# Router work of a fused attention and expert kernel: chosen behind the leaky passes, rows normalised at the end of a step, first expert products ahead of later takes

## The chip, the cores and the metric

One Trainium2 chip, one of its cores. The metric is the device time of one execution in microseconds. The core has five engines that run their own instruction queues in order and meet at semaphores: TensorE (PE in the profile), VectorE (DVE), ScalarE (ACT), GpSimd (POOL) and SyncE (SP), and 16 DMA engines.

## What is computed

A graph attention layer over 2048 nodes of width 128, then a layer of 64 experts of which each node uses two. Both add to their input.

```
x = x + attention(layernorm(x), adj)          # 2048 nodes, width 128
x = x + experts(layernorm(x))

attention: h = n @ W.T + b_W
           e[i,j] = leaky(h_i . a1 + h_j . a2 + b_a)     # slope 0.2
           softmax over j where adj[i,j] > 0, times h
experts:   logits = n @ Wr + br ; top 2 of 64 ; gates = softmax of the two
           out = sum over the two of gate * (relu(n @ W1[e] + b1[e]) @ W2[e] + b2[e])
```

## The kernel before

**Attention.** The nodes are 16 tiles of 128 (T = 16). Everything is unrolled, and each engine's order is written out by hand; the loop over s from 0 to 15 is a step on each engine. For tile s, VectorE makes the masked scores (L747), ScalarE their lower branch (`scores`, L560 to L564), VectorE the smaller of both in step s+1 (`leaky`, L753). TensorE transposes the result (`turn`, L1015) into four PSUM banks, ScalarE evacuates these with the exponential (`evac`, L576, four instructions, in its step s+1), TensorE multiplies by h (`attend`, L1039, 16 pairs of instructions with j from 0 to 15), and VectorE adds the result to x (`residual`, L757 and L761, in its step s+3). VectorE also makes the penalty of the next tile (L738). The scores live in a ring of three buffers, the transposed ones in a ring of two.

**Norm of the rows.** ScalarE sums the squared deviation of a finished tile (`deviation`, L583, step s-3). GpSimd makes from it the scale and shift of two tiles (`rstd_of`, L411 to L416, four operations, in even steps s). ScalarE writes the normalised rows twice (`norm`, L589). Before, tiles 2i and 2i+1 are normalised in step 5 + 2i, ahead of `evac`.

**Router.** The tiles form seven groups (START = 0, 4, 8, 10, 12, 14, 15, 16); LAST[q] is a group's last tile: 3, 7, 9, 11, 13, 14, 15. Per group: `route_a` on TensorE transposes the rows (L1049) and on ScalarE copies them out (L596); `route_b` on TensorE makes the logits (L1055, L1058) and on ScalarE one exponential (L601); `top2` on VectorE finds the two experts (first instruction L768, MAX8; last L782); `route_c` on TensorE ranks the nodes within their expert (L1078); `place` on VectorE makes gates and table positions (L789 to L800). GpSimd then writes each tile's rows into a table in memory, two indirect DMAs per tile (`place`, L431), in the steps that PLACED lists or after the loop, and loads the adjacency tiles (L377). `EARLY` is the number of groups handled inside the loop.

The order on VectorE in step s is

```
scores(s) ; penalty(s+1) ; residual(s-3) ; [top2(q) if s == LAST[q]+5] ; leaky(s-1) ; [place(q) if s == LAST[q]+5]
```

On ScalarE a step is scores(s), deviation(s-3), norms, route_b, evac(s-1), with the copy of route_a between the second and third bank of evac. On TensorE `route_a(q)` and `route_b(q)` stand at the start and a quarter into attend(LAST[q]+3), and `route_c(q)` ahead of turn(LAST[q]+4).

**Experts.** After the router, GpSimd gathers 34 blocks of 64 rows as 17 pairs (L480), TensorE transposes a gathered pair (`take`, L1135), ScalarE copies it out (`x_evac`, L649), and 96 steps, each one block with one expert, follow: `up` (L1146), relu halves on ScalarE (L654) and VectorE (L900), `down` (L1158), accumulation on VectorE (L907). ScalarE also copies the expert's weights (`fetch`, L662). `up(p)` waits until block pair min(p, 32)//2 + 1 has been copied out by `x_evac`. TensorE starts with take(0), take(1), up(0), up(1).

## Time and profile before

| | us |
|---|---|
| runs: median of 3 | 276.71 |
| runs: lowest, highest | 275.14, 277.4 |
| the profiled execution | 275.16 |
| its span, first to last instruction | 273.4 |
| mean granted TensorE clock | 0.926 of full |
| busy: TensorE, VectorE | 227.0, 208.4 |
| busy: ScalarE, GpSimd | 180.2, 167.0 |

The profile is of one execution. An engine is busy while an instruction of it runs; waits are not counted. Successive instructions of one engine overlap slightly, so the distance between two starts is what an instruction costs its engine. A wait is shown with the instruction that ended it. A row of a timeline gives start, duration, engine, line, operation, output and inputs, shape, count, and in brackets the idle time ahead of it with what ended it. A row of windows gives the stretch, its length, the busy time (and count of instructions) of TensorE, its weight loads, VectorE, ScalarE and GpSimd, the granted TensorE clock as a share of 2.4 GHz, the share of the DMA engines that was busy, and GB/s.

### The profile page before, as it was taken

To read this page: it belongs to the slowest core of one execution; us is meant where nothing else is said; L and a number is where in the kernel's file an instruction comes from. 1 tells how busy PE (TensorE), PEld (TensorE's weight loads), DVE (VectorE), ACT (ScalarE), POOL (GpSimd) and SP (SyncE) were. 2 spreads that over 40 slices of the span, in tenths; PEclk is the share of its full clock that TensorE was granted. 3 is DMA by queue.
4 is the path that set the end of the run, shared out by engine and by line. 5 is a ranking of instruction groups with operands and counts; after the bars stand their busy time and mean duration, and the time that the engine had idled before them with its cause. 6 is when DMAs were issued, how large, how long until landed. Compare 5 with 4: busy or idle time off the path is not lost.

```text
span 273.4 us, 6241 instructions
## 1 busy us (share of the span) xinstructions
PE 227.0 (83%) x1863; PEld 215.0 (79%) x1863; DVE 208.4 (76%) x587; ACT 180.2 (66%) x425; POOL 167.0 (61%) x212
## 2 busy tenths in 40 slices
PE   1494899999699966978884749999999999999840
PEld 1354899999689966978773639999999999999740
DVE  6879999996999799699455505889886766676465
ACT  2748989999298947758334336887877777777300
POOL 5770003450899889778577753455888888866500
PEclk9999799999799999799995557999999999999995
DMA  6988665589429817108931122222168701100067
GB/s 155 210 161 152 129 119 79 159 228 236 120 66 284 229 39 272 41 10 320 418 120 39 51 63 66 71 66 63 46 185 295 246 31 38 35 31 22 31 198 273
DMA packets 11120, 36.89 MB, mean 135 GB/s; under 512 B 2256, under 2 KB 2832, under 8 KB 10320
## 3 DMA queue, kind: packets, MB, share of 16 engines
q0 software_dynamic: 5232, 14.98, 24.1%
q1 hardware_dynamic: 5424, 21.11, 22.6%
q10 hardware_dynamic: 432, 0.40, 0.7%
q8 instruction: 17, 0.28, 0.4%
q14 instruction: 15, 0.12, 0.1%
HBM read 39.36 MB, written 5.51 MB: 164 GB/s over the span
## 4 chain that ended last, share of the span: by engine, by line
PE 60%; DVE 15%; POOL 7%; DMA 7%; issue 5%; ACT 3%; SPq 1%; POOLq 0%; DVEq 0%; ACTq 0%
PE bank L1146 17%; PE bank L1158 16%; PE bank L1039 12%; PE bank L1015 8%; DVE arena L753 5%; POOL table L431 5%; DMA xs<-in_x 2%; DMA arena<-result 2%; PE bank L980 2%; PE bank L1135 2%; PE bank L1058 1%; PE bank L1055 1%; DMA rows_in<-table,arena 1%; DVE idx L773 1%; DVE hot L779 1%
## 5 line engine op out<-in xcount | busy, mean ns | idle before, releaser
L1039 PE MATMUL bank<-arena 128*128 128x130 f32 x512 | 61.5, 276 | 0.0
L1146 PE MATMUL bank<-arena 128*128 x384 | 60.9, 283 | 0.1
L1039 PEld LDWEIGHTS bank<-arena 128*128 128x128 f32 x512 | 59.5, 192 | 0.5 <-ACT arena L576 0.3
L1158 PE MATMUL bank<-w2s,arena 128*128 x384 | 59.2, 277 | 0.2 <-issue 0.2
L431 POOL DMA_INDIRECT table<-rows_in,pos x32 | 48.7, 1522 | 8.9 <-issue 8.5
L1146 PEld LDWEIGHTS bank<-arena 128*128 128x128 f32 x384 | 52.0, 197 | 0.6 <-issue 0.3
L1158 PEld LDWEIGHTS bank<-w2s,arena 128*128 128x128 f32 x384 | 51.0, 193 | 0.6 <-issue 0.6
L907 DVE SCALAR_TENSOR_TENSOR arena<-bank,arena 128x128 f32 x96 | 33.6, 350 | 22.3 <-PE bank L1158 21.0
L654 ACT ACTIVATE arena<-bank,arena 128x128 f32<-128x128 f32 x96 | 35.1, 366 | 19.0 <-PE bank L1146 17.7
L1015 PE MATMUL bank<-ident,arena 128*128 128x128 f32 x256 | 35.5, 299 | 12.9 <-DVE arena L753 12.9
L576 ACT ACTIVATE arena<-bank 128x512 f32<-128x512 f32 x64 | 34.0, 597 | 14.9 <-PE bank L1015 14.6
L1015 PEld LDWEIGHTS bank<-ident,arena 128*128 128x128 f32 x256 | 32.0, 154 | 14.4 <-DVE arena L753 14.4
L662 ACT ACTIVATE arena<-arena 128x256 f32 x96 | 39.0, 408 | 2.3 <-issue 2.2
L494 POOL DMA_INDIRECT result<-arena x33 | 33.6, 1017 | 9.2 <-POOL arena L492 8.9
L900 DVE TENSOR_SCALAR arena<-bank,arena 128x128 f32<-128x128 f32 x96 | 33.2, 346 | 7.6 <-PE bank L1146 7.4
L753 DVE SCALAR_TENSOR_TENSOR arena<-arena,tneg 128x2048 f32<-128x2048 f32 x16 | 37.5, 2348 | 0.0
L747 DVE CUSTOM_DVE_ANT_0 arena<-arena 128x2048 f32<-128x2048 bf16 x16 | 36.7, 2301 | 0.9 <-ACT arena L516 0.9
L564 ACT ACTIVATE arena<-arena,c_lo 128x2048 f32<-128x2048 f32 x16 | 32.0, 2003 | 0.5
L480 POOL DMA_INDIRECT rows_in<-table,arena x17 | 16.1, 946 | 17.7 <-PE bank L1135 15.1
L377 POOL DMA_DIRECT2D arena<-in_adj x16 | 9.3, 584 | 26.0 <-DVE arena L738 25.7
L492 POOL TENSOR_SCALAR arena<-arena 128x128 f32<-128x128 f32 x32 | 19.6, 614 | 6.9 <-DVE arena L907 5.7
L411 POOL TENSOR_SCALAR nm<-total 128x2 f32<-128x2 f32 (+1 forms) x9 | 5.8, 649 | 16.5 <-ACT off L583 16.3
(195 smaller groups left out, 282.1 us busy)
## 6 DMA issues: line engine op xcount, KB each, us to landing
arena<-in_adj POOLq DMA_DIRECT2D x16, 512.0 KB, 6.6
w2s<-in_w SPq DMA_DIRECT2D x8, 768.0 KB, 4.5
arena<-in_w SPq DMA_DIRECT2D x6, 1024.0 KB, 9.3
arena<-in_w SPq DMA_DIRECT2D x4, 512.0 KB, 4.7
w2s<-in_w SPq DMA_DIRECT2D x4, 512.0 KB, 3.9
xs<-in_x SPq DMA_DIRECT2D x4, 256.0 KB, 6.5
arena<-result SPq DMA_DIRECT2D x2, 512.0 KB, 4.4
arena<-result SPq DMA_DIRECT2D x4, 256.0 KB, 5.9
```

The source lines that it names most:

```text
L431: pool.indirect_dma_start(table[:, :], bass.IndirectOffsetOnAxis(pos[:, t, k:k + 1], 0), rows_out[:, t, k, :].bitcast(I32), None).then_inc ...
L494: pool.indirect_dma_start(result[:, :], bass.IndirectOffsetOnAxis(slot_id[:, b:b + 1], 0), y_all[:, b, :], None).then_inc(e_put, 16)
L576: act.activation(pt_r[:, t % 2, CB * b:CB * b + CB, :].rearrange("p c i -> p (c i)"), bank[b][:, :], ACT.Exp, scale=-1.0).then_inc(s_ea, 1)
L654: act.activation(hT[:, p % UH, 0, :], hp(p, 0), ACT.Relu, bias=b1p[:, 0, p:p + 1]).then_inc(e_ha, 1)
L662: act.activation(w1u[:, p % UW, :], w1s[:, bass.ds(u, 1), :].rearrange("p e h -> p (e h)"), ACT.Copy).then_inc(e_w, 1)
L747: dve.tensor_tensor_reduce(out=z_r[:, t % 3, :], in0=pen[:, t % 2, :], in1=trow[:, :], scale=1.0, scalar=HIGHEST, op0=ALU.add, op1=ALU.min ...
L753: dve.scalar_tensor_tensor(z, z, tneg[:, t:t + 1], low(t), ALU.subtract, ALU.min).then_inc(s_lk, 1)
L907: dve.scalar_tensor_tensor(y, yp(p), mask[:, p:p + 1], y, ALU.mult, ALU.add).then_inc(e_acc, 1)
L1015: ins = pe.transpose(bank[b][:, P * c:P * c + P], z_r[:, t % 3, P * j:P * j + P], ident[:, :])
L1039: ins = pe.matmul(OB[t % 2][:, 0:D + 2], pt_r[:, t % 2, j, :], h[:, j, :], start=(j == 0), stop=(j == T - 1))
L1146: ins = pe.matmul(hp(p, b), w1u[:, p % UW, P * b:P * b + P], xT_all[:, bass.ds(column, P)], start=True, stop=True)
L1158: ins = pe.matmul(yp(p), hT[:, p % UH, b, :], w2s[:, bass.ds(u, 1), b, :].rearrange("p e d -> p (e d)"), start=(b == 0), stop=(b == HB - 1))
```

## The change

- `place(2, 8)` and `place(2, 9)` leave step 15 of GpSimd's loop; they go after the loop, one ahead of `rstd_of(6)` and one behind it. `EARLY` becomes 4, so group 3 is handled by the same loops.
- ScalarE normalises tiles s-4 and s-3 at the end of every even step s, after `evac(s-1)`: one step sooner than before. The copy of `route_a(q)` goes to step LAST[q]+4, after the deviation and ahead of `evac`; `route_b(q)` of ScalarE to the end of that step.
- VectorE runs `top2(q)` one step sooner (LAST[q]+4) and behind `leaky(s-1)` instead of ahead of it. `place(q)` stays in step LAST[q]+5 behind the leaky pass.
- TensorE runs `route_a(q)` at j = 8 of attend(LAST[q]+2), `route_b(q)` behind that product, and `route_c(q)` behind attend(LAST[q]+3).
- In the experts, TensorE runs take(0), up(0), up(1), take(1), down(0), up(2), take(2), and then the old loop from p = 1; ScalarE runs `x_evac(1)` behind `relu(0)`.

```diff
--- before.py
+++ after.py
@@ -23,9 +23,8 @@
     SLOT = [0, GRP, 0, 2, GRP, GRP + 2, GRP + 3]
     COUNTED = 2
     LAST = [START[q + 1] - 1 for q in range(NG)]
-    PLACED = [(0, 0, 9), (0, 1, 10), (0, 2, 11), (0, 3, 11), (1, 4, 13), (1, 5, 13), (1, 6, 13), (1, 7, 15), (2, 8, 15), (2, 9, 15)]
-    EARLY = 3
-    NORMED = [(5 + 2 * i, 2 * i) for i in range(5)]
+    PLACED = [(0, 0, 9), (0, 1, 10), (0, 2, 11), (0, 3, 11), (1, 4, 13), (1, 5, 13), (1, 6, 13), (1, 7, 15)]
+    EARLY = 4
     LNS = [(t, t + 2) for t in range(0, T - 2, 2)] + [(T - 2, T - 1), (T - 1, T)]
     CB = 4
     ROW = D + 2
@@ -456,7 +455,9 @@
                 for q in range(COUNTED):
                     if s == LAST[q] + 5:
                         counts(q)
+            place(2, 8)
             rstd_of(6)
+            place(2, 9)
             rstd_of(7)
             for t in (10, 11):
                 place(3, t)
@@ -565,9 +566,6 @@
 
             def evac(t):
                 for b in range(4):
-                    for q in range(NG):
-                        if b == 2 and q < EARLY and t == LAST[q] + 3:
-                            route_a(q)
                     if t == T - 1 and b == 2:
                         deviation(T - 2)
                     act.wait_ge(s_pt, 4 * t + b + 1)
@@ -608,20 +606,17 @@
                                   padrow[:, 1:1 + TOPK, :].rearrange("p j w -> p (j w)").bitcast(I32)).then_inc(d_tail, 16)
                 if s >= 3:
                     deviation(s - 3)
-                for at, t in NORMED:
-                    if s == at:
-                        norm(t)
-                        norm(t + 1)
                 for q in range(EARLY):
-                    if s == LAST[q] + 5:
-                        route_b(q)
-                if s == T - 1:
-                    route_a(3)
+                    if s == LAST[q] + 4:
+                        route_a(q)
                 if s >= 1:
                     evac(s - 1)
-                if s == T - 2:
-                    norm(T - 6)
-                    norm(T - 5)
+                if s >= 4 and s % 2 == 0:
+                    norm(s - 4)
+                    norm(s - 3)
+                for q in range(EARLY - 1):
+                    if s == LAST[q] + 4:
+                        route_b(q)
             deviation(T - 3)
             route_b(3)
             norm(T - 4)
@@ -668,9 +663,10 @@
                 fetch(p)
             act.wait_ge(s_b1, 1)
             x_evac(0)
-            x_evac(1)
             for p in range(PAIRS):
                 relu(p)
+                if p == 0:
+                    x_evac(1)
                 if p % 2 == 1 and p // 2 + 2 < NG2:
                     x_evac(p // 2 + 2)
                 if p + UW - 1 < PAIRS:
@@ -829,11 +825,10 @@
                     penalty(s + 1)
                 if s >= 3:
                     residual(s - 3)
-                for q in range(EARLY):
-                    if s == LAST[q] + 5:
+                leaky(s - 1)
+                for q in range(EARLY - 1):
+                    if s == LAST[q] + 4:
                         top2(q)
-                leaky(s - 1)
-                for q in range(EARLY):
                     if s == LAST[q] + 5:
                         place(q)
             leaky(T - 1)
@@ -1018,18 +1013,13 @@
             def attend(t):
                 if t >= 2:
                     pe.wait_ge(s_x1, t - 1)
-                for q in range(EARLY):
-                    if t == LAST[q] + 3:
-                        route_a(q)
-                if t == T - 2:
-                    route_b(3)
                 if t == T - 1:
                     route_a(4)
                 for j in range(T):
                     b = j // CB
                     for q in range(EARLY):
-                        if j == T // 4 and t == LAST[q] + 3:
-                            route_b(q)
+                        if j == 8 and t == LAST[q] + 2:
+                            route_a(q)
                     if t == T - 1 and j == 8:
                         route_b(4)
                     if t == T - 1 and j == 12:
@@ -1038,6 +1028,9 @@
                         pe.wait_ge(s_ea, 4 * t + b + 1)
                     ins = pe.matmul(OB[t % 2][:, 0:D + 2], pt_r[:, t % 2, j, :], h[:, j, :], start=(j == 0), stop=(j == T - 1))
                 ins.then_inc(s_o, 1)
+                for q in range(EARLY):
+                    if t == LAST[q] + 2:
+                        route_b(q)
 
             def route_a(q):
                 pe.wait_ge(s_row, START[q + 1])
@@ -1079,15 +1072,11 @@
                 ins.then_inc(s_rk, 1)
 
             for s in range(T):
-                for q in range(EARLY):
-                    if s == LAST[q] + 4:
-                        route_c(q)
                 turn(s)
                 attend(s)
-                if s == T - 3:
-                    route_a(3)
-                if s == T - 2:
-                    route_c(3)
+                for q in range(EARLY):
+                    if s == LAST[q] + 3:
+                        route_c(q)
             route_c(4)
             route_b(5)
             route_c(5)
@@ -1164,12 +1153,15 @@
             blocks = load_words(pe, "pe_b", 0, 0, WORDS)
             slots = load_words(pe, "pe_u", 1, 0, WORDS)
             take(0)
-            take(1)
             up(0)
             up(1)
+            take(1)
             pe.wait_ge(s_mask, 1)
             pe.wait_ge(s_b1, 1)
-            for p in range(PAIRS):
+            down(0)
+            up(2)
+            take(2)
+            for p in range(1, PAIRS):
                 if p % 2 == 0 and p // 2 + 2 < NG2:
                     take(p // 2 + 2)
                 if p + 2 < PAIRS:
```

## Rows read from the trace of the kernel before

**Rows 1.** Windows, the first four between starts of VectorE's steps (columns above).
```profile
55.25:60.81 5.56, 5.56 (x53) 5.56 (x52) 5.52 (x9) 5.44 (x10) 3.37 (x4) 1.00 0.93 254
60.81:74.11 13.30, 11.24 (x97) 10.47 (x97) 10.35 (x32) 8.43 (x17) 6.05 (x11) 0.93 0.65 151
...
90.90:103.39 12.49, 10.36 (x96) 9.47 (x95) 10.41 (x32) 8.02 (x18) 10.84 (x13) 1.00 0.43 115
...
109.07:120.67 11.60, 10.03 (x74) 9.66 (x75) 8.74 (x26) 7.02 (x15) 8.91 (x9) 0.85 0.10 30
...
72.10:75.60 3.50, 3.44 (x17) 3.44 (x18) 3.36 (x9) 1.79 (x3) 3.01 (x7) 0.52 0.65 216
```

**Rows 2.** Timeline of VectorE: start us, us, instruction [idle before <-releaser].
```profile
47.43 2.35 DVE L753 SCALAR_TENSOR_TENSOR arena<-arena,tneg 128x2048 f32<-128x2048 f32 x1
...
66.82 0.63 DVE L768 MAX8 top<-bank 128x8 f32<-128x64 f32 x4 [2.64 <-PE bank L1058]
...
69.76 2.35 DVE L753 SCALAR_TENSOR_TENSOR arena<-arena,tneg 128x2048 f32<-128x2048 f32 x1
72.02 0.16 DVE L789 TENSOR_SCALAR gs<-ge 128x4 f32<-128x4 f32 x1
...
74.11 2.40 DVE L747 CUSTOM_DVE_ANT_0 arena<-arena 128x2048 f32<-128x2048 bf16 x1
...
96.03 0.63 DVE L768 MAX8 top<-bank 128x8 f32<-128x64 f32 x4 [1.77 <-PE bank L1058]
...
114.99 0.36 DVE L768 MAX8 top<-bank 128x8 f32<-128x64 f32 x2 [2.55 <-PE bank L1058]
```

**Rows 3.** Timeline of ScalarE over one step and the norms of the next.
```profile
48.22 0.32 ACT L560 ACTIVATE r<-tneg,s 128x1 f32<-128x1 f32 x1
...
50.80 0.39 ACT L583 ACTIVATE off<-xs,total 128x128 f32<-128x128 f32 x1
...
51.19 1.08 ACT L589 ACTIVATE rows_in<-xs,nm,rstd 128x256 f32<-128x256 f32 x2
52.17 2.02 ACT L576 ACTIVATE arena<-bank 128x512 f32<-128x512 f32 x4
```

**Rows 4.** Timeline of TensorE: a clean step, group 0's router product, a later wait.
```profile
56.55 1.91 PE L1015 MATMUL bank<-ident,arena 128*128 128x128 f32 x16
58.29 3.75 PE L1039 MATMUL bank<-arena 128*128 128x130 f32 x32
61.87 1.91 PE L1015 MATMUL bank<-ident,arena 128*128 128x128 f32 x16
...
65.05 0.70 PE L1055 MATMUL bank<-bss,ones_f 1*128 1x256 f32 x2
...
135.51 0.41 PE L1049 MATMUL bank<-ident,rows_in 128*128 128x128 f32 x2 [1.12 <-issue]
```

**Rows 5.** Timeline of GpSimd: chains of statistics (L411 to L416) and table writes (L431).
```profile
47.98 1.86 POOL L416 TENSOR_TENSOR nm<-nm,rstd 128x2 f32<-128x2 f32 x1
...
74.55 2.98 POOL L431 DMA_INDIRECT table<-rows_in,pos  x1 [0.18 <-issue]
...
86.85 0.86 POOL L411 TENSOR_SCALAR nm<-total 128x2 f32<-128x2 f32 x1
...
89.18 1.85 POOL L416 TENSOR_TENSOR nm<-nm,rstd 128x2 f32<-128x2 f32 x1
...
131.69 0.96 POOL L431 DMA_INDIRECT table<-rows_in,pos  x1 [0.30 <-issue]
...
134.09 0.20 POOL L416 TENSOR_TENSOR nm<-nm,rstd 128x2 f32<-128x2 f32 x1
```

**Rows 6.** Timeline at the start of the experts, ScalarE and TensorE.
```profile
162.44 0.38 ACT L649 ACTIVATE arena<-bank 128x256 f32<-128x256 f32 x1 [0.16 <-PE bank L1135]
...
162.95 0.69 PE L1135 MATMUL bank<-ident,rows_in 128*128 128x128 f32 x2 [0.60 <-DMA rows_in<-table,arena]
...
163.43 1.91 PE L1146 MATMUL bank<-arena 128*128 x8
```

## The prediction

> **What bounds the kernel now.** I read the busy shares first, then the busy time between the starts of VectorE's steps, then each engine's timeline over two such steps, and last the chain of waits. Over 20 to 129 us the kernel runs 16 attention steps, and VectorE sets their pace. A step without router work lasts 5.56 us, with VectorE busy for 5.52 of it, TensorE for 5.56 and ScalarE for 5.44 [rows 1]: three engines are nearly full, VectorE has no slack, and neither of the others can make up much. A leaky pass costs 72.02 - 69.76 = 2.27 us of it [rows 2]; scores (2.2), penalty and residual make up the other 3.3. The three steps with a routed group are the long ones: 13.30, 12.49 and 11.60 us [rows 1]. VectorE waits in them for the logits: 2.64, 1.77 and 2.55 us ahead of the first MAX8 [rows 2], 6.96 in all. Its own router work is 69.76 - 66.82 = 2.94 us for the choice and 74.11 - 72.02 = 2.09 for the placing of four tiles [rows 2], which the change moves but does not shorten. TensorE's step is a turn (1.75 us) and an attention product (3.58): 5.33 us from 56.55 to 61.87 [rows 4]. ScalarE's step is 2.6 for scores, 0.4 for the deviation and 1.9 for four evacuations, 4.9 us; two norms add 1.0 us every second step [rows 3]. So ScalarE needs 10.8 us of every 11.1. GpSimd looks idle at first, but from 74.5 us on it is a queue of table writes [rows 5].
>
> **Part 1, the norms moved to the end of the even steps (ScalarE).** Before, the statistics of a pair were made on GpSimd one whole step ahead of the norms. Now norm(s-4) and norm(s-3) stand in the very step whose deviation(s-3) starts GpSimd's chain. That chain has four operations; for tiles 0 and 1 the last of them starts at 47.98, 0.55 us into a leaky pass of VectorE (47.43 to 49.70), and takes 1.86 us, to 49.84 [rows 2, 5]. The same operation takes 0.20 where no leaky pass runs, at 134.09 [rows 5]. ScalarE's evacuations end at 48.22 [rows 3], so it now stands until 49.9, and norms to 50.9. What is queued behind the wait: the next scores, the evacuation of the next turn, and through it TensorE's product. In numbers: scores(5) start at 50.9 instead of 48.22, its last result is ready at 53.55, so leaky(5) starts 0.6 late (VectorE could at 47.43 + 5.55 = 52.98); evac(4) starts at 53.94 instead of 52.17 [rows 2, 3], and attend(4) 0.7 behind it at 54.7.
>
> The Trainium skill (SBUF — State Buffer, "SBUF: two separate sides") says that VectorE and GpSimd share a pair of ports as an exclusive lock, and that a VectorE operation with two SBUF inputs, as the leaky pass is, blocks a GpSimd operation that reads SBUF until it ends. The trace agrees (1.86 us against 0.20). With the lock the first norm wait is 1.7 us, without it 0.
>
> **Part 2, the choice of group 0 behind leaky(6).** I follow it on. leaky(5) ends at 55.87, leaky(6) at 61.42. attend(4) ends at 58.25, turn(5) runs to 60.0, evac(5) on ScalarE from 58.9 to 60.8, deviation(3) ends at 58.9. GpSimd's chain for tiles 2 and 3 begins at 59.0, meets leaky(6) (59.15 to 61.42) and ends at about 62.7; norm(3) is done at 63.7. TensorE stands in the middle of attend(5) (its eighth tile is reached at 61.8) for these rows until 63.85, transposes (0.44), ends the product at 66.1. ScalarE's copy of the transposed rows stands behind scores(7) (2.6) and deviation(4) (0.4 to 0.5): 63.7 + 3.1 + 0.5 = 67.3. Then the router product, begun at 65.05 before and followed by the MAX8 at 66.82, 1.75 us [rows 2, 4]: 69.1. VectorE, free at 61.4, starts top2(0) at 69.1: it waits 7.7 us where it waited 2.64. From there 2.94 + 5.55 + 2.09 gives 79.7 for the start of step 9, which was 74.11 [rows 2]. **Group 0: +5.6 us.** TensorE's next turn and product lie beside this, hence the cover that the change uses; but VectorE, not TensorE, is what later steps wait for, so that cover gives nothing back.
>
> **Part 3, group 1.** It is the same chain, but GpSimd now comes to the statistics of tiles 6 and 7 only after four table writes and two adjacency loads. Before, these ran from 74.55 to 86.85, and the chain from there to 91.03 (89.18 + 1.85) [rows 5]; I keep the 12.3 us, because a write beside a busy VectorE takes up to 2.98 against 0.96 beside an idle one [rows 5]. Place(0) now ends at 79.7; GpSimd still counts group 0, so the writes start at 81.1, the chain at 93.4, it ends at 97.6 behind leaky(10). ScalarE would be free at 93.5 and stands 4.1 us. Norms to 98.6, scores(11) and deviation(8) and the copy to 102.1, router product to 103.8. VectorE has ended leaky(10) at 96.4: it waits 7.5 us (1.77 before). Step 13 starts at 103.9 + 2.94 + 5.55 + 2.09 = 114.5 instead of 103.39 [rows 1]. **Group 1: +5.5.**
>
> **Part 4, group 2.** Here place(1) (2.09) stands between the leaky pass that frees the turn and the choice, GpSimd is idle, and the group has two tiles. By the same chain the logits are ready 1.2 us after leaky(12) instead of 2.55 late: step 15 starts at 130.3 instead of 120.67 [rows 1], +9.6 in all. **Group 2: -1.5.**
>
> **Part 5, group 3 and the table writes moved.** The norms of tiles 10 and 11 wait for GpSimd behind the six writes of tiles 4 to 6 (114.8 to 130.0 by 3.2 us each beside a busy VectorE and 1.26 beside an idle one), which costs TensorE another 1.4 us in the product of tile 13. Moving place(2, 9) behind rstd_of(6) takes two writes of 1.26 from ahead of norm(12), and the 1.12 us for which TensorE stood ahead of route_a(4) at 135.51 vanish [rows 4]. It comes there at 145.3 and, with its product no longer held up behind it, to route_b(4) 9.5 later than before. From there nine writes of GpSimd, the last being the padding, set the end as before. **Tail: -0.1.**
>
> **Part 6, the experts' start.** take(1) waited for its gathered block until 162.95 and up(0), up(1) began at 163.43 [rows 6]. Now up(0) needs only x_evac(0), which started at 162.44 and took 0.38 [rows 6], so it starts at 162.9. The transposes of takes 1 and 2 are the same work, later in the queue. down(0) moves ahead of up(2) and take(2): relu(0) is long done, and relu(1) behind x_evac(1) is done before down(1). The fifth gather waits for take(1), some 1.8 us later than now, and its block is wanted only by take(4), four expert steps on. The loop after it is bound by TensorE, so what is gained at the start stays. **-0.5** (0 if ScalarE's new order costs it, -1 if the slow stretch, in which eight products take 1.91 us [rows 6], also ends sooner).
>
> **Sum.** 275.16 (the profiled execution, of which 273.4 is the span) + 5.6 + 5.5 - 1.5 - 0.1 - 0.5 = 284.2. The median of the runs, 276.71, is 1.55 above that execution; I take half of it and predict 285.0.
>
> **Clock.** TensorE waited for the choice of group 0 and for leaky(7), and the next turn was granted 0.52 (near 1.2 GHz): 3.44 us busy instead of 1.75 [rows 1, 4]. With the same waits around group 1 the clock stayed at 1.00 [rows 1]. The new waits of TensorE (2.0 and 1.3 us at group 0, 4.0 and 1.3 at group 1) may halve the router product's speed: up to 1.6 us for each of two groups. I take 0 in the sum and +3.2 as the upper bound.
>
> [...]
>
> **Rivals.** A: *GpSimd's chain is not held up* (the leaky pass misses it, or writes are quicker). Then only ScalarE's order counts: norm(3) ends at 60.4, copy at 64.0, logits at 65.7, and group 0 costs +2.2; group 1 at 3.5 us of waiting against 1.77 costs +1.7; with -1.3, -0.1 and -0.5 the time is 277.2. The rows with 1.86 and 2.98 us [rows 5] speak against it. B (the other side): *the choice is ready almost when the leaky pass ends*, as it would be were ScalarE never late. TensorE alone needs 1.75 + 3.58 + 0.6 + 1.75 = 7.7 us from a leaky pass, against VectorE's 5.55: waits of 2.1, 2.1 and 0 instead of 6.96 in all, so -2.8, and -0.5: 271.9. It decides from the point at which group 0's logits come before 61.4 + 2.64 = 64.0. The 3.1 us of scores and deviation ahead of the copy [rows 3] speak against it: even a norm that waits for nothing gives 64.0 for the copy alone. C: *the changes of order cancel*, waits about as long as before: 274 to 279. D: *the clock falls too*: 287 to 289.
>
> **Chances.** My forecast (281 to 287) 0.52; A (277 to 281) 0.20; C 0.10; D 0.11; B 0.07. The range leaves out B, half of C and the far end of D: 277.0 to 289.0. A measurement of this kernel tells 1% (2.8 us) from no change: over 1% faster takes B, 0.07; within 1% takes C and a small part of A, 0.14; slower 0.79.
>
> **What would show it.** In the changed kernel's trace: VectorE's idle time ahead of the first MAX8 of groups 0 and 1 at 5 to 8 us each and about 1 for group 2; ScalarE idle ahead of L589's norms, released by GpSimd, for 1 to 2 us at first and about 4 in step 10; a gap in TensorE's product of step 5. If those norms wait for nothing, part 1 is wrong and A holds. If the MAX8 waits add up to less than 7 us, the forecast is wrong in sign. An up(0) that does not start before the second take makes part 6 nothing.

## The result, and the profile after

The changed kernel takes 287.25 us (median of 4 runs, 285.59 to 289.4) against 275.92 before: a ratio of 1.0451, 95% interval 1.0313 to 1.0589. It is slower, as forecast; 285.0 was predicted, with 277 to 289. Here and below a median takes all runs of a kernel, while a ratio leaves out those more than 1.5% above its fastest. Its profiled execution took 285.81 us, with a span of 284.0 against 273.4, so 10.6 us are to be found between two traces.

VectorE first, as in [rows 2]: its timeline in the changed kernel (start us, us, instruction, in brackets the wait ahead of it and what ended it). L743 is the scores, L749 the leaky pass, L764 the choice.

```profile
47.57 2.38 DVE L749 SCALAR_TENSOR_TENSOR arena<-arena,tneg 128x2048 f32<-128x2048 f32 x1
49.87 2.28 DVE L743 CUSTOM_DVE_ANT_0 arena<-arena 128x2048 f32<-128x2048 bf16 x1
...
53.72 2.35 DVE L749 SCALAR_TENSOR_TENSOR arena<-arena,tneg 128x2048 f32<-128x2048 f32 x1 [0.48 <-ACT arena L565]
...
68.86 0.63 DVE L764 MAX8 top<-bank 128x8 f32<-128x64 f32 x4 [7.22 <-PE bank L1051]
...
79.54 2.28 DVE L743 CUSTOM_DVE_ANT_0 arena<-arena 128x2048 f32<-128x2048 bf16 x1
...
103.37 0.63 DVE L764 MAX8 top<-bank 128x8 f32<-128x64 f32 x4 [6.99 <-PE bank L1051]
...
114.07 2.28 DVE L743 CUSTOM_DVE_ANT_0 arena<-arena 128x2048 f32<-128x2048 bf16 x1
...
121.60 0.36 DVE L764 MAX8 top<-bank 128x8 f32<-128x64 f32 x2 [1.80 <-PE bank L1051]
...
130.59 2.28 DVE L743 CUSTOM_DVE_ANT_0 arena<-arena 128x2048 f32<-128x2048 bf16 x1
...
136.95 2.35 DVE L749 SCALAR_TENSOR_TENSOR arena<-arena,tneg 128x2048 f32<-128x2048 f32 x1 [1.33 <-ACT arena L565]
```

The waits for the logits are 7.22, 6.99 and 1.80 us where [rows 2] has 2.64, 1.77 and 2.55: 16.0 in place of 7.0. The start of step 9 is 79.54 against 74.11 (0.17 of the difference was there at step 6 already), that of step 13 114.07 against 103.39, that of step 15 130.59 against 120.67.

What ends those waits is read on ScalarE and TensorE. First ScalarE's timeline in the changed kernel.

```profile
50.03 1.10 ACT L587 ACTIVATE rows_in<-xs,nm,rstd 128x256 f32<-128x256 f32 x2 [0.89 <-POOL nm L415]
...
62.53 1.09 ACT L587 ACTIVATE rows_in<-xs,nm,rstd 128x256 f32<-128x256 f32 x2 [1.49 <-POOL nm L415]
...
66.46 0.57 ACT L594 ACTIVATE x2T<-bank 128x512 f32<-128x512 f32 x1
...
96.47 1.09 ACT L587 ACTIVATE rows_in<-xs,nm,rstd 128x256 f32<-128x256 f32 x2 [2.84 <-POOL nm L415]
```

And TensorE's:

```profile
63.67 0.66 PE L1042 MATMUL bank<-ident,rows_in 128*128 128x128 f32 x4 [1.63 <-ACT rows_in L587]
...
67.09 0.70 PE L1048 MATMUL bank<-bss,ones_f 1*128 1x256 f32 x2 [0.96 <-ACT x2T L594]
...
97.61 0.66 PE L1042 MATMUL bank<-ident,rows_in 128*128 128x128 f32 x4 [2.98 <-ACT rows_in L587]
98.11 3.42 PE L1029 MATMUL bank<-arena 128*128 128x130 f32 x16
...
112.00 3.62 PE L1010 MATMUL bank<-ident,arena 128*128 128x128 f32 x16 [2.93 <-DVE arena L749]
...
145.91 0.38 PE L1042 MATMUL bank<-ident,rows_in 128*128 128x128 f32 x2
```

Group 0 reads as a chain: the norms wait for GpSimd (L415) until 62.53, TensorE stands in the middle of its product until 63.67 for these rows, the copy (L594) comes only at 66.46 behind the scores and the deviation, and TensorE waits for it again. In [rows 3] no norm waited. At 98.11 the second half of the product takes 3.42 us where 1.96 is usual, and the turn at 112.00 3.62 against the 1.91 of [rows 4]. The windows between VectorE's steps (columns as in [rows 1]) show the granted clock of these stretches at 0.87 to 0.89; over the slow product alone (98.11 to 101.53) it is 0.54, over the slow turn (112.00 to 115.62) 0.53:

```profile
90.74:106.32 15.58, 12.60 (x93) 11.71 (x92) 8.42 (x25) 8.92 (x19) 9.44 (x10) 0.89 0.63 172
106.32:114.07 7.75, 4.82 (x45) 4.69 (x45) 7.58 (x16) 3.64 (x7) 1.97 (x6) 0.87 0.13 28
```

GpSimd's timeline has the cause of the first waits. L413 is the power and L415 the product that ends the statistics, the one of 47.98 in [rows 5].

```profile
47.61 0.72 POOL L413 TENSOR_TENSOR rstd<-ve,expo 128x2 f32<-128x2 f32 x1
48.41 1.59 POOL L415 TENSOR_TENSOR nm<-nm,rstd 128x2 f32<-128x2 f32 x1
...
59.58 2.64 POOL L413 TENSOR_TENSOR rstd<-ve,expo 128x2 f32<-128x2 f32 x1
62.30 0.20 POOL L415 TENSOR_TENSOR nm<-nm,rstd 128x2 f32<-128x2 f32 x1
```

The experts start like this on TensorE, with the last `down` product of the stage; [rows 6] has the same place before.

```profile
171.65 0.69 PE L1124 MATMUL bank<-ident,rows_in 128*128 128x128 f32 x2 [3.00 <-DMA rows_in<-table,arena]
173.15 2.07 PE L1135 MATMUL bank<-arena 128*128 x8 [0.81 <-ACT arena L644]
...
178.91 0.71 PE L1135 MATMUL bank<-arena 128*128 x4 [0.27 <-ACT arena L657]
...
266.57 0.71 PE L1147 MATMUL bank<-w2s,arena 128*128 x4 [0.20 <-issue]
```

The first take is at 171.65 against 161.66 (+10.0) and the last product at 266.57 against 256.10 (+10.5). So the router's part costs 10.0 and the experts' start another 0.5; the last 0.1 of the 10.6 come behind the last product.

### The profile page after: what moved, and what is told of

It reads as the page before. It is cut to its first block, busy times and chain, and to the rows that moved or that the text cites. A ratio compares the mean times of both kernels' runs of the same rounds, so it can differ in the third digit from the quotient of the medians.

```text
span 284.0 us, 6243 instructions
## 1 busy us (share of the span) xinstructions
PE 229.9 (81%) x1863; PEld 218.5 (77%) x1863; DVE 208.7 (73%) x587; ACT 180.5 (64%) x425; POOL 156.7 (55%) x212
## 4 chain that ended last, share of the span: by engine, by line
PE 51%; DVE 12%; POOL 11%; issue 9%; ACT 8%; DMA 7%; SPq 1%; POOLq 0%; ACTq 0%; DVEq 0%
PE bank L1135 16%; PE bank L1147 15%; PE bank L1029 6%; PE bank L1010 6%; POOL table L430 4%; DVE arena L743 3%; DVE arena L749 2%; DMA xs<-in_x 2%; DMA arena<-result 2%; ACT rows_in L587 2%; POOL rstd L413 2%; PE bank L975 2%; ACT arena L574 2%; PE bank L1051 2%; PE bank L1124 1%
## 5 line engine op out<-in xcount | busy, mean ns | idle before, releaser
L1029 PE MATMUL bank<-arena 128*128 128x130 f32 x512 | 64.0, 283 | 1.0 <-ACT arena L574 1.0
L1029 PEld LDWEIGHTS bank<-arena 128*128 128x128 f32 x512 | 62.3, 199 | 1.2 <-issue 1.2
L1135 PEld LDWEIGHTS bank<-arena 128*128 128x128 f32 x384 | 51.4, 195 | 2.4 <-issue 2.2
L1010 PE MATMUL bank<-ident,arena 128*128 128x128 f32 x256 | 37.3, 309 | 13.2 <-DVE arena L749 13.2
L430 POOL DMA_INDIRECT table<-rows_in,pos x32 | 41.2, 1289 | 8.8 <-issue 8.3
L1010 PEld LDWEIGHTS bank<-ident,arena 128*128 128x128 f32 x256 | 34.0, 161 | 14.2 <-DVE arena L749 14.2
L749 DVE SCALAR_TENSOR_TENSOR arena<-arena,tneg 128x2048 f32<-128x2048 f32 x16 | 37.6, 2350 | 1.8 <-ACT arena L565 1.8
L743 DVE CUSTOM_DVE_ANT_0 arena<-arena 128x2048 f32<-128x2048 bf16 x16 | 36.5, 2285 | 0.3 <-ACT arena L517 0.3
L764 DVE MAX8 top<-bank 128x8 f32<-128x64 f32 x16 | 2.8, 222 | 21.0 <-PE bank L1051 21.0
(195 smaller groups left out, 281.5 us busy)
```

The costliest lines, as they stand in the source:

```text
L430: pool.indirect_dma_start(table[:, :], bass.IndirectOffsetOnAxis(pos[:, t, k:k + 1], 0), rows_out[:, t, k, :].bitcast(I32), None).then_inc ...
L743: dve.tensor_tensor_reduce(out=z_r[:, t % 3, :], in0=pen[:, t % 2, :], in1=trow[:, :], scale=1.0, scalar=HIGHEST, op0=ALU.add, op1=ALU.min ...
L749: dve.scalar_tensor_tensor(z, z, tneg[:, t:t + 1], low(t), ALU.subtract, ALU.min).then_inc(s_lk, 1)
L1010: ins = pe.transpose(bank[b][:, P * c:P * c + P], z_r[:, t % 3, P * j:P * j + P], ident[:, :])
L1029: ins = pe.matmul(OB[t % 2][:, 0:D + 2], pt_r[:, t % 2, j, :], h[:, j, :], start=(j == 0), stop=(j == T - 1))
L1135: ins = pe.matmul(hp(p, b), w1u[:, p % UW, P * b:P * b + P], xT_all[:, bass.ds(column, P)], start=True, stop=True)
```

## The experiments

**The two halves of the change.** Is the loss in the router alone, and does the new start of the experts bring or cost something? Two kernels: the one before with the experts' edit (on TensorE as below, and `x_evac(1)` behind `relu(0)` on ScalarE), and the changed one without it.

```diff
             take(0)
-            take(1)
             up(0)
             up(1)
+            take(1)
...
+            down(0)
+            up(2)
+            take(2)
-            for p in range(PAIRS):
+            for p in range(1, PAIRS):
```

> The kernel before with only the experts' new start (take(1) behind up(1), down(0), up(2), take(2), x_evac(1) behind relu(0)). Read within the expert stage, from the start of the first take to the last down product: 94.44 us before, 94.92 in the changed kernel. Theory: ScalarE, which now copies block 1 between relu(0) and the weight copies, falls behind, up(4) waits for a weight copy (0.27 us in the changed kernel) and the stage takes 94.8 to 95.0. Rival, the prediction's part 6: the stage takes 93.9, and the 0.48 us lost in the changed kernel came from the phase in which the router work left the stage. The first MAX8 waits stay at 2.64, 1.77 and 2.55.

Measured: from the first take at 162.40 to the last product at 257.65 it is 95.25 us, against 256.10 - 161.66 = 94.44 before. The start costs 0.8 us, a little more than the theory's 0.4 to 0.6, and the rival's gain of 0.5 is excluded. The kernel took 276.92 us (one execution). The waits ahead of the first MAX8 were 3.24, 2.97 and 2.55 in this execution, so those of the kernel before vary by over a microsecond as well.

> The changed kernel with the old start of the experts, so the router's part alone. Theory: all of the slowdown but 0.5 us is here; its profiled span is 283.3 to 283.8, the ratio to the kernel before 1.035 to 1.045, and VectorE waits 7.2, 7.0 and 1.8 us ahead of the first MAX8 of groups 0, 1, 2. Rival (the experts' start costs some of the loss by its order and by a clock that rises later): ratio 1.02 to 1.03.

Measured: 289.1 us against 277.26, ratio 1.0433 (1.0352 to 1.0515), and 94.45 us from first take to last product, as before. So the router's part carries the slowdown. The profiled span missed, 288.9 instead of 283.3 to 283.8 (it is the longest of the four runs, 287.57 to 290.66): VectorE waited 5.87, 6.41 and 1.25 us for the logits, but 2.67 and 3.76 ahead of two leaky passes for which the changed kernel's profile has 0.48 and 1.33. That opened a question of its own, taken up with e10 and e11.

TensorE's timeline of e1 shows where the start loses: the first products begin 1.49 us behind the first take (1.77 before, [rows 6]), and then `up(4)` waits for a weight copy on ScalarE, which now copies a gathered block between `relu(0)` and its weight copies. That is only part of the 0.8 us: the instruction ahead, `up(3)` at 168.52, is already 0.51 us late, 6.12 us behind the first take against 167.27 - 161.66 = 5.61 before. The lower clock lasted longer here. The granted clock was 0.50 and 0.54 over `up(2)` and the take behind it, which took 1.01 and 0.40 us from start to start; in the changed kernel it was 0.67 and 1.00 there, and they took 0.77 and 0.22.

```profile
163.89 2.07 PE L1147 MATMUL bank<-arena 128*128 x8 [0.81 <-ACT arena L649]
...
167.11 1.22 PE L1147 MATMUL bank<-arena 128*128 x4
168.12 0.57 PE L1136 MATMUL bank<-ident,rows_in 128*128 128x128 f32 x2
...
170.07 0.71 PE L1147 MATMUL bank<-arena 128*128 x4 [0.27 <-ACT arena L662]
```

**Which part of the chain makes the wait.** The forecast had GpSimd's statistics and ScalarE's order in series. One kernel takes away what the norms wait for, one moves the copy, one does both.

```diff
             def norm(t):
+                if t < 12:
+                    act.activation(rows_out[:, t, :, 0:D],
+                                   xs[:, t, :].rearrange("p (k d) -> p k d", k=1)
+                                   .to_broadcast([P, TOPK, D]), ACT.Identity,
+                                   bias=lift[:, 0:1], scale=1.0).then_inc(s_row, 1)
+                    return
                 act.wait_ge(s_nm2, t // 2 + 1 if t < T - 1 else T // 2 + 1)
```

> The changed kernel in which the rows of tiles 0 to 11 are copied with a constant shift and scale 1 instead of the layer norm's (that part of the computation is left out), so ScalarE's norms inside the loop wait for nothing from GpSimd; GpSimd still makes its statistics. Theory (two causes in series, GpSimd's chain and ScalarE's order): the norm waits of 0.9, 1.5 and 2.8 us vanish, and VectorE's waits ahead of the first MAX8 fall from 7.2 and 7.0 to 4.3 to 5.0 and 3.5 to 4.5, group 2's stays at 1 to 1.8; the kernel comes out 4 to 6 us under the changed one. Rival (ScalarE's order alone sets the wait): the waits fall by less than 1 us each. Rival (GpSimd alone): they fall to 2.1, what TensorE alone needs.

Measured: waits of 4.34, 4.71 and 1.20 us, span 277.1 (278.88 us), 6.9 under the changed kernel and more than expected, since leaky(5) is no longer held either and leaky(15) only by 0.34. Group 1's 4.71 lies just above the expected 4.5. Between these two executions GpSimd's statistics account for about two thirds of the loss of 10.6.

```diff
             for s in range(T):
+                for q in range(EARLY):
+                    if s == LAST[q] + 4:
+                        route_a(q)
                 scores(s)
...
-                for q in range(EARLY):
-                    if s == LAST[q] + 4:
-                        route_a(q)
                 if s >= 1:
                     evac(s - 1)
```

> The changed kernel in which ScalarE copies the transposed rows at the start of its step, ahead of scores and deviation instead of behind them. Theory: in group 0 the copy moves from 66.46 to about 64.3 but TensorE then has to end its product (66.0) before the logits, so they come 1.0 us sooner, VectorE's wait is 6.2 instead of 7.2; group 1 likewise, where the second half of the product ran at the low clock to 101.46 and the copy was done by 101.0: no gain, 7.0. Group 2: about 1.0 less. In all 1 to 2.5 us under the changed kernel. Rival (the copy behind the scores is the main cause): 2 us less in each of two groups, 4 us or more in all.

Measured: 6.18 and 6.89, as expected for groups 0 and 1; 1.87 in group 2, where a shorter wait was expected and none came. The span is 281.5 (283.23 us), 2.5 under the changed kernel; only 1.1 of this is in the two waits for the logits, and 1.8 arise from step 15 to the first take (39.29 us against 41.06), which the expectation did not have. The copy's place matters, but behind late norms it can give little.

> The changed kernel with both earlier edits: norms of tiles 0 to 11 with a constant shift and scale (the layer norm of these rows is left out), and the copy of the transposed rows ahead of the scores on ScalarE. Theory: the two causes stand in series, so with both gone only TensorE's own order is left: VectorE waits 2.5 to 3.5 us ahead of the first MAX8 of groups 0 and 1 and 0 to 1 in group 2, which is still more than the kernel before waits, and the span is about 273 to 275. Rival (a further cause): the waits stay above 4.

Measured: span 272.2 (273.96 us), a little under the expected 273 to 275, and waits 3.80, 2.24 and 0.67 (the bracketed numbers of VectorE's timeline, here of e3 and then e7):

```profile
65.43 0.63 DVE L769 MAX8 top<-bank 128x8 f32<-128x64 f32 x4 [4.34 <-PE bank L1056]
...
97.68 0.63 DVE L769 MAX8 top<-bank 128x8 f32<-128x64 f32 x4 [4.71 <-PE bank L1056]
```

```profile
63.78 0.62 DVE L769 MAX8 top<-bank 128x8 f32<-128x64 f32 x4 [3.80 <-PE bank L1056]
...
93.53 0.62 DVE L769 MAX8 top<-bank 128x8 f32<-128x64 f32 x4 [2.24 <-PE bank L1056]
```

Their sum is 6.7 us, within 0.3 of the kernel before: with both causes gone, the order of the changed kernel has gained nothing that shows in these waits. (Two other executions of the router as it was before, in e1 and e8, have 8.8 and 9.1, so a gain of some 2 us can't be excluded from one execution.) The span is 11.8 under the changed kernel, more than the 6.9 and 2.5 of the two edits alone, as two causes in series would give it. Group 0's 3.80 missed the expected 2.5 to 3.5. There TensorE never stood for rows: it started turn(5) at 56.09, 1.8 us behind the end of leaky(5), since it still worked off what it was behind, and then its turn, product and logits took their full time. This is the floor that rival B of the prediction put at 2.1.

**How long GpSimd's statistics take.** In the changed kernel the power (L413) started 0.04 us behind the start of a leaky pass and took 0.72; in e2 it started 0.05 behind one and took 2.88. Two looks: one small instruction more on GpSimd ahead of that power, and the changed kernel once more.

```diff
                 pool.wait_ge(s_ve2, i + 1)
+                if i == 0:
+                    pool.tensor_scalar(spare[:, :], pidx[:, :], 2.0, None, ALU.mult)
```

> The changed kernel with one small instruction more on GpSimd, 128x1 elements, ahead of the power of rstd_of(0) (L413 in the changed kernel), some 0.2 us. In the changed kernel that power started 0.04 us into a leaky pass and took 0.72; in e2 it started 0.05 us into it and took 2.88. Theory (a GpSimd instruction that comes once a leaky pass is under way stands until the pass ends): the power now starts 0.2 to 0.3 us into leaky(4) and takes over 2 us, the norm of tiles 0 and 1 waits 2.5 to 3.2 us instead of 0.89, leaky(5) 2 to 2.7 instead of 0.48, and step 7 starts 1.5 to 2.3 us later. Rival (the long power of e2 had another cause): the norm waits 1.1 us, 0.2 more than before.

Measured: 291.38 us, span 289.6. GpSimd's timeline in e10:

```profile
47.47 2.39 POOL L415 TENSOR_SCALAR spare<-pidx 128x1 f32<-128x1 f32 x1
49.82 2.80 POOL L416 TENSOR_TENSOR rstd<-ve,expo 128x2 f32<-128x2 f32 x1
```

VectorE's in e10 (L752 leaky, L746 scores):

```profile
47.43 2.35 DVE L752 SCALAR_TENSOR_TENSOR arena<-arena,tneg 128x2048 f32<-128x2048 f32 x1
49.69 2.28 DVE L746 CUSTOM_DVE_ANT_0 arena<-arena 128x2048 f32<-128x2048 bf16 x1
...
56.61 2.35 DVE L752 SCALAR_TENSOR_TENSOR arena<-arena,tneg 128x2048 f32<-128x2048 f32 x1 [3.55 <-ACT arena L568]
```

The small instruction itself stood until the leaky pass had ended, 2.39 us for 128 numbers, and the power behind it fell into the next scores pass and took 2.80. The norm waited 3.94 us, leaky(5) 3.55, and step 7 began at 58.88 instead of 55.98: a delay of 2.9 us, above the 2.3 expected, from an instruction of a few tenths. The direction and the cause are the theory's; its size was taken too small because I had not counted the scores pass as a second one to stand behind.

> The changed kernel once more, to see how far its waits vary by themselves. Theory: VectorE's waits ahead of the first MAX8 stay within 1.5 us of 7.2, 7.0 and 1.8, their sum with the waits of leaky(5) and leaky(15) is 16 to 21 us, and the time follows that sum. Rival: the waits are the same to 0.2 us and the spread of the runs lies elsewhere.

Measured: 289.55 us, span 287.8, with waits of 5.87, 6.54 and 1.62 for the logits and 2.68 and 3.76 ahead of leaky(5) and leaky(15): 20.5 in all where the first profile has 17.8. GpSimd's timeline there:

```profile
46.56 2.88 POOL L413 TENSOR_TENSOR rstd<-ve,expo 128x2 f32<-128x2 f32 x1
```

And VectorE's:

```profile
46.51 2.35 DVE L749 SCALAR_TENSOR_TENSOR arena<-arena,tneg 128x2048 f32<-128x2048 f32 x1
```

The same program thus falls into a short or a long case. The recorded start of the power does not tell which: at 0.05 us into a leaky pass it took 0.72 us in e1 and e5 and 2.88 in e2 and e11, at 0.04 it took 0.72 in the changed kernel's first profile and 2.88 in e8. What settles it within these hundredths stays open.

The first power makes only part of the 3.8 us of span. Counted from the first scores, step 15 comes 1.1 us later in e11; another 3.0 lie between step 15 and the first take, 44.07 us against 41.06 (the first scores come 0.6 sooner). There GpSimd meets the passes a second time. The fifth of the six table writes of step 13 began at 123.46 in the first profile, 0.02 us ahead of a scores pass, and took 0.96; in e11 it began 0.18 into that pass and took 2.94. The sixth took 3.05 instead of 1.89, the power of tiles 10 and 11 2.86 instead of 0.72, and ScalarE's norms waited 3.75 for it where they had waited for nothing. This is behind the 3.76 ahead of leaky(15), 1.33 in the first profile. e2 and e10 have long waits ahead of both passes too (2.67 and 3.76, 3.55 and 3.76), e4 has neither (0.47 and 0.78). Whether the first meeting brings about the second is not shown.

TensorE's timeline in e11 at group 1 shows one more difference: behind the same wait of 2.98 us the second half of the product takes 1.96 us, at a granted clock of 1.00, and not 3.42.

```profile
98.78 0.65 PE L1042 MATMUL bank<-ident,rows_in 128*128 128x128 f32 x4 [2.98 <-ACT rows_in L587]
99.27 1.96 PE L1029 MATMUL bank<-arena 128*128 128x130 f32 x16
```

**The same idea, without taking the step away.** If only VectorE's waits count, the leaky pass can cover them while everything else keeps its step.

```diff
+                leaky(s - 1)
                 for q in range(EARLY):
                     if s == LAST[q] + 5:
                         top2(q)
-                leaky(s - 1)
-                for q in range(EARLY):
-                    if s == LAST[q] + 5:
                         place(q)
```

> The kernel before with one edit: in VectorE's step LAST+5 the leaky pass runs first and the choice and the placing behind it, everything else as it was (norms, products and copies keep their steps). Theory (what VectorE waits for is the logits, and only its own sum of work and waits sets the pace): the leaky pass of 2.27 us covers the wait; ahead of the first MAX8 0.3 to 0.6, 0 and 0.2 to 0.4 us are left instead of 2.64, 1.77, 2.55, and about 0.5 us per group is new ahead of the ranks' product (L794); step 15 starts 4.5 to 5.3 us sooner. TensorE stands longer ahead of its turn and catches up. Of this 2 to 4.5 us reach the end, because GpSimd loses the quiet stretches in which it writes the table fast. Rival (GpSimd's queue is the bound ahead of norm(12)): less than 1 us reaches the end. Rival (TensorE's later turn makes it the bound): VectorE waits 1 to 2 us in the steps behind each group and the gain is 0.

Measured: the waits fell to 0.99, 0 and 0 us, with 0.19 new ahead of the ranks' product in groups 0 and 1 where 0.5 was expected. From the first scores to step 15 it is 95.1 us against 100.1, so 5.0 gained between two executions (it is 102.2 in e1 and 102.6 in e8, whose router is that of the kernel before). But the kernel takes 274.29 against 275.26, ratio 0.9961 (0.9922 to 1.0): the first rival was right on the end. GpSimd's timeline in e5:

```profile
115.10 2.89 POOL L431 DMA_INDIRECT table<-rows_in,pos  x1 [0.30 <-issue]
118.02 1.97 POOL L411 TENSOR_SCALAR nm<-total 128x2 f32<-128x2 f32 x1
```

ScalarE's in e5:

```profile
121.35 1.09 ACT L589 ACTIVATE rows_in<-xs,nm,rstd 128x256 f32<-128x256 f32 x2 [5.04 <-POOL nm L416]
```

VectorE's in e5:

```profile
125.02 2.35 DVE L753 SCALAR_TENSOR_TENSOR arena<-arena,tneg 128x2048 f32<-128x2048 f32 x1 [5.12 <-ACT arena L564]
```

The sixth write of step 13 ends at 118.0, only then can the statistics of tiles 10 and 11 start, ScalarE's norms wait 5.04 us for them, and VectorE's last leaky pass 5.12 for ScalarE: what was gained is given back.

The next two kernels move table writes. The change's own move is put to the kernel before and to e5; then writes are put behind the statistics that are waited for.

```diff
-(1, 7, 15), (2, 8, 15), (2, 9, 15)]
+(1, 7, 15)]
...
+            place(2, 8)
             rstd_of(6)
+            place(2, 9)
             rstd_of(7)
```

> The kernel before with only the table writes of tiles 8 and 9 moved as in the changed kernel. Theory: rstd_of(6) comes about 2.5 us sooner, the 1.12 us for which TensorE stands ahead of route_a(4) vanish, the two writes fill GpSimd's idle 2.56 us; the span from the start of step 15 to the first take is 0.8 to 1.2 us shorter than 40.99. Rival: the later writes push the end of the table, and nothing is gained.

Measured: from the start of step 15 at 122.08 to the first take at 161.34 it is 39.26 us against 40.99, so 1.7 shorter: more than expected, because group 4's first MAX8 waits 2.79 instead of 4.69. The 40.99 is steady: e1, with the old writes, has 162.40 - 121.41 = 40.99 too. Within its stretch this part of the change pays. The whole kernel took 274.44 us in its one execution, inside the spread of the kernel before (273.02 to 277.42).

> The last kernel with the changed kernel's other move as well: the table writes of tiles 8 and 9 leave step 15 and stand around the statistics of tiles 12 and 13. Theory: GpSimd no longer holds norm(12); 4 to 5.5 us under the kernel before, ratio 0.980 to 0.986. Rival (the writes only come later and set the end): the same as the kernel without this move, or slower.

Measured: 270.23 against 275.26 us, ratio 0.9804 (0.9744 to 0.9865), span 267.7. The six runs go from 268.49 to 274.31, and the ratio leaves out the upper two. The theory's 0.980 to 0.986 was met.

> e6 beside e9 on one chip. Theory: ratio to the kernel before again 0.974 to 0.987, and above e9's by 0.002 to 0.007.

Measured: 272.39 against 275.11 us, 268.9 to 275.11 over its runs. Its profile (275.11 us, span 273.4) shows the 5.04 and 5.11 us of e5 again; the first profile of e6 had 1.11 and 1.01 there. The ratio, 0.9798 (0.9754 to 0.9841), leaves out three of the six runs, 273.94, 274.67 and 275.11 us, of which the last is the profiled one. They belong to the kernel all the same, and in them it is no faster than e5, whose ten runs lie at 271.53 and from 273.75 to 275.04. (That the other long runs of e6 have the same wait is not shown: they have no trace.) By the medians e6 is at 0.982 of the kernel before here and 0.990 in e12. The expected order of the ratios missed: e12's is 0.002 below e9's and not 0.002 to 0.007 above.

```diff
-(1, 6, 13), (1, 7, 15)]
+(1, 6, 15), (1, 7, 15)]
...
-            place(2, 8)
             rstd_of(6)
+            place(2, 8)
             place(2, 9)
```

> The kernel e6 with GpSimd's order changed once more: the table writes of tile 6 go from step 13 to step 15, and those of tiles 8 and 9 both stand behind rstd_of(6). Theory (what e5 lost again and e6 kept in part is GpSimd's statistics waiting behind its own table writes): the norms of tiles 10 and 11 wait for nothing or under 1.2 us, leaky(15) is not held, norm(12) comes 1 to 1.5 us sooner; 0.5 to 2 us under e6, and the runs lie closer together. Rival (the writes are only put off to where they set the end of the table): no gain or 1 us slower than e6.

Measured: 269.75 against 275.11 us, ratio 0.9819 (0.9788 to 0.9851), with all six runs between 268.81 and 270.82. The norms of tiles 10 and 11 (118.07 below) wait for nothing, and no leaky pass waits. VectorE's timeline in e9, the choice of groups 2 and 3:

```profile
112.79 0.36 DVE L770 MAX8 top<-bank 128x8 f32<-128x64 f32 x2 [0.26 <-PE bank L1058]
124.93 0.36 DVE L770 MAX8 top<-bank 128x8 f32<-128x64 f32 x2 [0.25 <-PE bank L1058]
```

ScalarE's in e9:

```profile
118.07 1.11 ACT L591 ACTIVATE rows_in<-xs,nm,rstd 128x256 f32<-128x256 f32 x2
...
128.23 1.09 ACT L591 ACTIVATE rows_in<-xs,nm,rstd 128x256 f32<-128x256 f32 x2 [2.45 <-POOL nm L416]
```

By its ratio it is no faster than e6, and the expected 0.5 to 2 us under e6 holds for the medians alone (269.75 against 270.23 and 272.39, so 0.5 and 2.6): none of its six runs has the length of those with the 5 us wait. norm(12) came at 128.23, hardly sooner than e6's 128.55, so there the gain of 1 to 1.5 us was not had. This kernel beats both the one before and the changed one, by 5.4 and 17.5 us of median. Each beside its own runs of the kernel before, their ratios are 0.9819 and 1.0451.

## Why the prediction was right, point by point

- **What bounds the kernel.** VectorE's sum of work and waits: right. Step 13 starts 10.7 us later than before, and of these 9.8 are longer waits for the logits of groups 0 and 1, 0.48 is leaky(5)'s and 0.17 was there at step 6, which leaves 0.2 to everything else.
- **Part 1.** The norm waits were forecast as 1.7 and 1.9 us and measured as 0.89 and 1.49, leaky(5) 0.6 late and measured 0.48. Right in place; the size depends on when GpSimd meets the leaky pass, as e11 (3.06 in the first) and e10 (3.94) showed. The first wait was about half the forecast in this execution and nearly twice it in e11.
- **Part 2, group 0.** The times on the way were forecast within 0.3 us: the first MAX8 at 69.1 (68.86), the start of step 9 at 79.7 (79.54). The waits were forecast less closely, the norm's 1.9 against 1.49 and VectorE's 7.7 against 7.22, and two errors cancelled: the norms were done 0.2 sooner and the start of the attention 0.17 later.
- **Part 3, group 1.** Step 13 was forecast at 114.5 and came at 114.07, for reasons that partly differ. GpSimd's writes began at 82.88 and not 81.1, since two small sums of its count had taken 2.77 us and not the 0.69 of the kernel before. The four writes and two loads then took 9.4 us (82.88 to 92.25) and not 12.3: the first write began 0.04 us ahead of a leaky pass and took 1.13 instead of 2.98, the second 1.82 instead of 2.90. So ScalarE stood 2.84 and not 4.1. Against that, TensorE after its wait of 2.98 us ran the second half of the product at the lower clock, 3.42 instead of 1.96 us, for which I had put 0 into the sum. In e11 the same product behind the same wait took 1.96, so this cost does not come in every execution. The Trainium skill (TensorE: Matmul & The Clock Gate, "Why this matters for your kernels") names idle gaps of TensorE as a cause of lower throughput. The traces agree only in part: slow stretches do stand behind waits, but the length of the wait alone does not tell which, by e11 and by the rows of the last section.
- **Part 4, group 2.** Forecast -1.5, measured 16.52 - 17.28 = -0.76, since turn(11) took 3.62 us at the lower clock and the logits came 1.80 and not 1.2 late (VectorE's wait 0.75 us shorter than before, and not 1.35).
- **Part 5, the tail.** From the start of step 15 to the first take 41.06 against 40.99: +0.07 where -0.1 stood. TensorE came to route_a(4) at 145.91, forecast 145.3. The way there was another, and that it came out so close is luck: the norms of tiles 10 and 11 waited for nothing, where they were to wait for GpSimd's six writes, and instead leaky(15) waited 1.33 us. In e11 those norms did wait, 3.75 us, and the stretch took 44.07.
- **Part 6, the experts.** This term failed in sign: -0.5 forecast, +0.5 in the changed kernel, +0.8 in e1. I followed TensorE's queue and not ScalarE's: its copy of block 1, now behind `relu(0)`, pushes the weight copies back, and `up(4)` waits for one. The products also began 1.50 us behind the first take instead of 1.77, a gain of 0.27 and not of 0.5, and `up(3)` had lost it again, in e1 with a lower clock that lasted longer.
- **The rivals.** A (GpSimd's chain not held up) is nearest to the kernel e3, which took 278.88 us where 277.2 was worked out (group 1 waited 4.71 and not 3.5); the changed kernel isn't it. B's condition was not met in either profile of the changed kernel: group 0's first MAX8 started at 68.86 and 70.00, not before 64.0. D, the clock, came in part: half a product of group 1 and three turns were slow (3.33, 3.62 and 3.56 us), where the kernel before has two such turns (3.63 and 3.16). The median of 287.25 lies in D's band of 287 to 289, just above the 281 to 287 of the main forecast; the stated range covers both. C is excluded.
- **The sum.** 284.2 for the profiled execution, measured 285.81; 285.0 for the median, measured 287.25. The 1.6 us of the profiled execution are the experts' 1.0, group 2's 0.7, 0.2 in the tail and 0.1 behind the last product, less the 0.4 by which groups 0 and 1 cost less than forecast (5.4 and 5.25 against 5.6 and 5.5). The clock is not a term beside these: its cost lies within groups 1 and 2 and the experts, and in group 1 GpSimd's quicker writes made up for it. The median is another 0.6 above its forecast, because two of the four runs, 288.69 and 289.40 us, are as long as e11, whose longer waits are traced above.

## What to carry to other kernels

Work moved one step sooner is only hidden if all that feeds it is sooner as well: follow the chain through every in-order queue it crosses, here statistics on GpSimd, norm and copy on ScalarE, transposes and logits on TensorE. Where one engine sets the pace, swap its own instructions so that the wait falls behind work that is ready, and leave the feeding chain in its step. Then look at what has been late-but-covered: here GpSimd's table writes, which had run fast in just those stretches in which VectorE used to wait, and which gave back 4 of 5 us in e5. Moving those of tiles 8 and 9 won it back in only some executions (e6), moving tile 6's as well, and tile 8's behind the statistics, in all six runs (e9).

## What was not expected of the hardware

- GpSimd stands while a long VectorE pass with two operands in SBUF runs, for the leaky pass and the scores pass alike. The last operation of the statistics takes 0.19 to 0.20 us alone and 1.59 to 2.14 beside a pass, the power 0.71 to 0.74 alone and up to 2.88 beside one, a product over 128 numbers 2.39 (e10). The Trainium skill (SBUF — State Buffer, "SBUF: two separate sides") states this lock for a VectorE operation with two SBUF inputs against a GpSimd operation that reads SBUF, and the traces agree. What I had not expected is how little decides it: a power with a recorded start 0.04 or 0.05 us into a leaky pass took 0.72 us in some executions and 2.88 in others, and the same kernel had spans of 284.0 and 287.8 us, in part from this.
- Issuing an indirect DMA on GpSimd (the table writes) stretches in the same way, 0.96 us in a quiet stretch and up to 3.06 beside those passes. Issuing a plain load of the adjacency (L377) does not: 0.53 to 0.74 us in the loops of all runs. A fixed number of table writes so costs more, the less VectorE waits.
- The length of TensorE's wait does not tell by itself whether the granted clock is low behind it. In the changed kernel it was not low after waits of 0.96 and 1.63 us, and was low after those of 2.93, 2.98 and 2.15 (turns of 3.33, 3.62 and 3.56 us for 1.9, half a product of 3.42 for 1.96). But e11 has a product at the full clock behind 2.98, and the kernel before has two turns behind waits of 1.68 us, one of 3.63 us (at 72.16) and one of 1.97 (at 101.44). What decides between them these traces do not show.
